# A two-layer graph kernel on one core: the front's order redrawn on all five engines

## The reference

```python
deg = max((adj != 0).sum(-1), 1)
h = relu(layernorm(x))
hs = h @ W_sa;  s_left = hs @ a_sa[0, :D];  s_right = hs @ a_sa[0, D:]
e = where(adj != 0, exp(-leaky_relu(s_left[:, None] + s_right[None, :], 0.01)), 0)
x_a = (e / (e.sum(1) + 1e-5)) @ hs
x_b = adj @ (h @ W_g) + b_g
gate_a = sigmoid(concat(adj @ h, h) @ Wa.T + ba)
gate_b = sigmoid(concat(adj @ h, h) @ Wb.T + bb)
x = x + sigmoid(gate_a * x_a + gate_b * x_b)
h = relu(layernorm(x))
dinv = rsqrt(deg)
x = x + relu((dinv * (adj + I) * dinv @ h + h) @ W1 + b1)
```

## Time and profile before

| | us |
|---|---|
| three runs | 601.46, 602.61, 606.09; median 602.61 |
| profiled execution, whole time | 602.26 |
| its span, first to last instruction | 600.5 |
| PE busy | 583.7 |
| DVE busy | 509.6 |
| ACT busy | 374.4 |
| POOL busy | 213.2 |

### The profile page before, as it was taken

How to read it: one execution, slowest core, us unless ns; L and a number is a source line. 1 busy time by engine, 2 the same in 40 slices (tenths; PEclk the granted TensorE clock), 3 DMA queues, 4 the chain that set the end, 5 groups by cost and what they waited for, 6 DMA issues and landing times.

```text
span 600.5 us, 14573 instructions
## 1 busy us (share of the span) xinstructions
PE 583.7 (97%) x5841; PEld 507.1 (84%) x5841; DVE 509.6 (85%) x965; ACT 374.4 (62%) x899; POOL 213.2 (35%) x319
## 2 busy tenths in 40 slices
PE   6889999999999999999999999999999999999996
PEld 4446778888888888888888888888888889999995
DVE  5897795999999999899989989988782999988852
ACT  3677776798979788888888879889770331000000
POOL 3655323453545444443444358223131323000001
PEclk9999999999999999999999999999999999999999
DMA  7908299776574647474756475000130266656511
GB/s 199 225 8 115 71 190 238 184 107 173 77 185 76 171 72 175 73 175 72 176 76 172 76 169 77 6 18 2 20 114 19 72 258 221 203 184 205 185 34 36
DMA packets 55807, 73.69 MB, mean 123 GB/s; under 512 B 20027, under 2 KB 47933, under 8 KB 54331
## 3 DMA queue, kind: packets, MB, share of 16 engines
q0 software_dynamic: 28544, 22.15, 26.9%
q1 hardware_dynamic: 24754, 46.42, 23.7%
q10 hardware_dynamic: 2441, 4.20, 2.5%
HBM read 69.31 MB, written 22.16 MB: 152 GB/s over the span
## 4 chain that ended last, share of the span: by engine, by line
PE 78%; DVE 6%; POOL 5%; issue 4%; DMA 4%; ACT 2%; ACTq 0%; POOLq 0%; DVEq 0%
PE accE L860 11%; PE accE L862 11%; PE accE L861 11%; PE accA L838 11%; PE accA L839 10%; PE accA L946 4%; PE accA L945 4%; DMA stage<-in_adj_dram 3%; PE accE L946 2%; PE accE L945 2%; PE accA L904 2%; PE accA L905 2%; POOL stage L420 1%; DVE bst L1052 1%; DMA late<-in_L_gnn_W_gcnb_dram 1%
## 5 line engine op out<-in xcount | busy, mean ns | idle before, releaser
L860 PE MATMUL accE<-HI,Z 128*128 128x257 f16 x676 | 184.3, 273 | 1.3 <-DVE wm L1197 0.9
L862 PE MATMUL accE<-HI,E 128*128 128x257 f16 x676 | 184.1, 272 | 0.0
L861 PE MATMUL accE<-LO,Z 128*128 128x256 f16 x676 | 183.9, 272 | 0.0
L594 ACT ACTIVATE Z<-LO,sr 128x256 f32<-128x256 f32 x338 | 151.4, 497 | 32.8 <-PE accE L862 32.8
L838 PE MATMUL accA<-HI,adjT 128*128 128x260 f16 x676 | 154.0, 273 | 0.0
L839 PE MATMUL accA<-LO,adjT 128*128 128x258 f16 x676 | 154.0, 273 | 0.0
L603 ACT ACTIVATE Z<-Z,sr 128x256 f32<-128x256 f32 x338 | 150.1, 496 | 0.2
L1153 DVE TENSOR_TENSOR Z<-adjT,Z 128x512 f32<-128x512 bf16 x169 | 126.0, 745 | 17.1 <-ACT Z L603 16.1
L1159 DVE TENSOR_TENSOR E<-Z 128x512 bf16<-128x512 f32 x169 | 128.7, 762 | 5.8
L420 POOL DMA_DIRECT2D stage<-in_adj_dram x96 | 59.3, 649 | 90.6 <-DVE adjT L1145 86.3
L860 PEld LDWEIGHTS accE<-HI,Z 128*128 128x128 bf16 x676 | 65.8, 97 | 10.5 <-issue 1.5
(11 more groups left out here) (208 smaller groups left out, 1081.7 us busy)
## 6 DMA issues: line engine op xcount, KB each, us to landing
adjT_store<-adjT SPq DMA_DIRECT2D x11, 1664.0 KB, 6.3
stage<-in_adj_dram POOLq DMA_DIRECT2D x48, 192.0 KB, 5.0
stage<-in_adj_dram POOLq DMA_DIRECT2D x36, 224.0 KB, 5.1
adjT<-adjT_store SPq DMA_DIRECT2D x7, 896.0 KB, 5.8
adjT<-adjT_store SPq DMA_DIRECT2D x7, 768.0 KB, 7.1
stage<-adjT_store SPq DMA_DIRECT2D x4, 896.0 KB, 6.2
stage<-adjT_store SPq DMA_DIRECT2D x4, 768.0 KB, 7.0
out_dram<-late ACTq DMA_DIRECT2D x11, 256.0 KB
```

The lines of the kernel that those rows point to most:

```text
L594: ins = act.activation(Z[:, n % RING, v], slw[:, m], ACT.Relu, bias=sr99[:, t:t + 1], scale=1.0 - SLOPE)
L860: pe.matmul(dst[:, 0:D + 1], zhi, HI[:, t, 0:D + 1], start=(t == 0), stop=False)
L861: pe.matmul(dst[:, 0:D], zhi, LO[:, t, 0:D], start=False, stop=False)
L862: ins = pe.matmul(dst[:, 0:D + 1], zlo, HI[:, t, 0:D + 1], start=False, stop=(t == TILES - 1))
```

## The change

It redraws the first 90 us or so, on every engine, and leaves the sums as they are.

- **Score columns.** The four DVE reductions of W_sa with a_sa are gone, and the 256 KB load that spread a_sa. PE transposes W_sa (4), ACT copies it, PE multiplies it by a_sa's four columns (4 small matmuls), DVE copies two columns. a_sa, Wa and Wb come as 12 rows, issued by POOL.
- **One statistic a step.** `BATCHES` is gone; POOL makes the power of pair s + 3 in step s, DVE `minus_mean(s + 2)`.
- **Turns between a dense product's tiles.** PE's `dense(i)` has `turn(i + 1)` between its two tiles, and ACT and DVE take the tiles' halves one by one. `project(s)` follows dense(s). The first product (`dense_first`) begins before the weights' second halves are there. Filler matmuls go from 60 to 32.
- **W1's scale later.** The scales of W_sa, W_g and the gate rows come in one go; that of W1 in steps 14 to 17, and its halves after round 0's gates. W1's load and that of the gate biases are issued after x.
- **Gate biases early.** POOL makes `nbias` in step 5 instead of behind the issues of chunk (3,0).
- **Adjacency.** Chunk (0,0) is turned in two parts in steps 5 and 7, (0,1) in step 9, (1,0) in 11, (1,1) in 13; chunks (1,0), (1,1), (2,0) are issued in POOL's steps 8, 10, 12 (before 6, 7, 11), (2,1) behind the loop. `turn_adj(2, 0)` moves behind round 0's gates and W1's halves, `turn_adj(2, 1)` from u = 4 to u = 6 of round 1.

```diff
-            for k, w in enumerate((ba, bb)):
-                sp.dma_start(bias2[:, k:k + 1], ...).then_inc(bias_in, 16)
-            sp.dma_start(w1, W1.rearrange("(h p) o -> p h o", p=P)).then_inc(w1_in, 16)
             sp.wait_ge(wsg_in, 32)
...
             sp.dma_start(b1rep[:], bass.AP(b1.tensor, 0, [[0, P], [1, D]])).then_inc(rep_in, 16)
+            for k, w in enumerate((ba, bb)):
+                sp.dma_start(bias2[:, k:k + 1], ...).then_inc(bias_in, 16)
+            sp.dma_start(w1, W1.rearrange("(h p) o -> p h o", p=P)).then_inc(w1_in, 16)
...
@@ POOL
+            for k, w in enumerate((Wa, Wb, a_sa)):
+                pool.dma_start(wrows[4 * k:4 * k + 4, :], w.rearrange("o (r p) -> (o r) p", p=P)).then_inc(wrows_in, 16)
...
-            inv_stds(2)
             score_weight_parts()
+            inv_std(2)
+            inv_std(3)
             load_adj(0, 1)
-            loads = {6: (1, 0), 7: (1, 1), 11: (2, 0), 12: (2, 1)}
+            loads = {8: (1, 0), 10: (1, 1), 12: (2, 0)}
             for s in range(PAIRS):
                 score_parts(s)
-                if s == 0:
-                    inv_stds(3)
-                if s in (0, 1, 2, 4):
-                    inv_stds({0: 4, 1: 5, 2: 6, 4: 7}[s])
                 gate_columns(s)
+                if 1 <= s and s + 3 < PAIRS:
+                    inv_std(s + 3)
+                if s == 5:
+                    pool.wait_ge(bias_in, 32)
+                    pool.tensor_scalar(nbias[:], bias2[:], -1.0, None, ALU.mult).then_inc(nbias_ok, 1)
                 if s in loads:
                     load_adj(*loads[s])
+            load_adj(2, 1)
...
@@ ACT
-                if 0 < s < PAIRS:
-                    first_halves(s)
+                if 0 <= s - 6 < PAIRS:
+                    expo(0, s - 6)
+                if s < PAIRS:
+                    first_half(s, 0)
                 if s + 1 < PAIRS:
                     turned(s + 1)
                 if s + 2 < PAIRS:
                     norm(s + 2)
+                if s < PAIRS:
+                    first_half(s, 1)
...
@@ PE
             def dense(i):
...
                     ins.then_inc(dn_ps, 1)
+                    if e == 0 and i + 1 < PAIRS:
+                        turn(i + 1)
...
+            turn_first_weights()
             turn(0)
-            keep_busy(20)
-            for s in range(PAIRS):
+            spread_weights(accE, 0, 3, 1)
+            score_columns()
+            keep_busy(8)
+            turn(1)
+            dense_first()
+            project(0)
+            for s in range(1, PAIRS):
                 dense(s)
...
+                project(s)
                 if s >= 6:
                     neighbours(0, s - 6)
                 if s >= 7:
                     unit(0, s - 7)
-                if s + 1 < PAIRS:
-                    project(s + 1)
...
@@ DVE
             for s in range(1, PAIRS + 6):
+                if s < PAIRS:
+                    second_half(s, 0)
+                if s + 2 < PAIRS:
+                    minus_mean(s + 2)
+                if s + 1 < PAIRS:
+                    turned_second(s + 1)
                 if s < PAIRS:
                     take_scores(s)
+                if s + 3 < PAIRS:
+                    row_stats(s + 3)
+                if s < PAIRS:
+                    second_half(s, 1)
...
-            turn_adj(2, 0)
             gate_args(0)
             gates(0)
+            second_weights(2)
+            turn_adj(2, 0)
```

More of the change, by code:

```diff
@@ L510, in _ @@
             load_adj(3, 0)
-            pool.wait_ge(bias_in, 32)
-            pool.tensor_scalar(nbias[:], bias2[:], -1.0, None, ALU.mult).then_inc(nbias_ok, 1)
             with_bias(0)
@@ L801, in widen_first, with dense_first @@
                           stop=True).then_inc(wide, 1)
+            def dense_first():
+                pe.wait_ge(whi_ok, 2)
+                pe.wait_ge(hTh_ok, 1)
+                for e in range(2):
+                    rows = slice(e * P, (e + 1) * P)
+                    for h in range(HALVES):
+                        pe.matmul(bank(dn, e), hTh[:, 0, h, rows], wh[:, h], start=(h == 0), stop=False)
+                    pe.wait_ge(hTl_ok, 1)
+                    for h in range(HALVES):
+                        pe.matmul(bank(dn, e), hTl[:, 0, h, rows], wh[:, h], start=False, stop=False)
+                    pe.wait_ge(wlo_ok, 2)
+                    for h in range(HALVES):
+                        ins = pe.matmul(bank(dn, e), hTh[:, 0, h, rows], wl[:, h], start=False,
+                                        stop=(h == HALVES - 1))
+                    ins.then_inc(dn_ps, 1)
             def dense(i):
-                if i == 0:
-                    pe.wait_ge(wlo_ok, 2)
                 pe.wait_ge(hTl_ok, i + 1)
                 for e in range(2):
-                    if i >= 1:
-                        pe.wait_ge(lo_ok, 2 * i - 1 + e)
+                    pe.wait_ge(lo_ok, 2 * i - 1 + e)
                     rows = slice(e * P, (e + 1) * P)
@@ L1057, in row_stats, with minus_mean @@
                 ins.then_inc(stats, 1)
-            def minus_mean(n):
-                a, b = BATCHES[n]
-                dve.wait_ge(rstd_ok, n + 1)
-                dve.scalar_tensor_tensor(out=nmr[:, a:b], in0=mv[:, a:b, :, 0], scalar=-1.0, in1=rstd[:, a:b],
+            def minus_mean(i):
+                dve.wait_ge(rstd_ok, i + 1)
+                dve.scalar_tensor_tensor(out=nmr[:, i], in0=mv[:, i, :, 0], scalar=-1.0, in1=rstd[:, i],
                                          op0=ALU.mult, op1=ALU.mult).then_inc(nmr_ok, 1)
             def score_weights():
-                dve.wait_ge(wsg_in, 32)
-                dve.wait_ge(arep_in, 16)
-                for h in range(HALVES):
-                    for k, dst in enumerate((w6[:, 3, h:h + 1], w6[:, 0, h:h + 1])):
-                        dve.tensor_tensor_reduce(out=prod[2 * h + k], in0=wsg[0][:, h, :],
-                                                 in1=arep[:, k * D:(k + 1) * D], scale=1.0, scalar=0.0, op0=ALU.mult,
-                                                 op1=ALU.add, accum_out=dst).then_inc(wprep, 1)
+                dve.wait_ge(wscore, 1)
+                columns = pw[:, 16:20].rearrange("p (h k) -> p k h", k=2)
+                dve.tensor_copy(w6[:, 3], columns[:, 0]).then_inc(wprep, 1)
+                dve.tensor_copy(w6[:, 0], columns[:, 1]).then_inc(wprep, 1)
             def largest(k0, k1):
@@ L1234, in _ @@
             row_stats(1)
+            gate_weights()
+            largest(2, 3)
+            minus_mean(0)
             dve.wait_ge(wsg_in, 32)
             largest(0, 1)
[L1237 removed]
             largest(1, 2)
[L1239 removed]
             minus_mean(1)
[L1241 to L1243 removed]
+            on_diagonal(0, 3)
+            scales(accE, 0, 3, 1)
+            score_weights()
+            turned_second(0)
             second_weights(0)
[L1245 removed]
@@ L1278, in _ @@
                 if s in turns:
                     turn_adj(*turns[s])
+                if s == 14:
+                    dve.wait_ge(w1_in, 16)
+                    largest(3, 4)
+                    on_diagonal(3, 4)
+                if s == 17:
+                    scales(pw, 3, 4, 2)
                 if 0 <= s - 6 < PAIRS:
```

197 lines of the change are left out of this document (96 added, 101 removed).

## The result

The changed kernel took 612.83 us in the median of four executions (607.06 to 612.85), the kernel before 602.32 beside it: a ratio of 1.0144, 95% interval 1.0113 to 1.0176. It is slower by more than the 1% that a measurement of this kernel tells apart, and outside the range of the forecast. A second series of five gave 606.4 (605.13 to 615.73), ratio 1.0063 (1.0041 to 1.0085). The ratio leaves out the execution of 615.73, a slow one by its distance from the fastest.

What follows compares the result with a forecast made beforehand. PE bounds the kernel, busy 583.7 of 600.5 us, so only gaps and useless work can be won. 7.8 of the front plus 1.1, less 3.0 and 4.4, gives 1.5 (1.4 by the times): 601.0 us, range 596.0 to 608.0.

Steps and rivals of the forecast that it cites:

- the front: Up to round 1's `neighbours`: 86.5 us instead of 94.25, 7.8 us won, with dense(0) at 12.4 and dense(8) at 45.0.
- the second score store: In SP's line: 10.6 us from block 0's landing at 92.2, so block 1 is stored at 114.5 and DVE waits 6.1.
- three signs of being wrong: DVE reaching the transpositions without waiting (then (A)), a score store of 15 us or more (then (B)), dense(8) after 48 (then (C)).
- The last sum: Forecast time: 600.9 us against the profiled execution, median 0.35 above the profiled one, given as 601.0.
- round 2 at 134.2: Start of round 2, before at 135.63: `unit(1,8)` at 117.7 plus 16.5 for the rest of round 1.
- the step without `rstd`: Front, dense(3) to dense(4), 18.9 to 24.4: DVE stands at `minus_mean(4)` since POOL holds `inv_std(4)` behind issues and columns.
- the quiet price: 10.6 us for a score store, instead of the crowded 18.3; the second was taken to meet only the loads of block 3.
- DVE waits 6.1: Before block 2's transposition: DVE stands ready at 86.1 and waits 6.1 us for block 0's store, landed at 92.2.
- `unit(1,0)` at 101.0: Start of round 1's units on PE: 5.8 us earlier than before, PE having stood 3.0.
- (B): Rival: score stores share the engines with adjacency loads, block 1 landing after 115.9; 611.8 us, chance 0.14.
- (C): Rival: the front wins 4 instead of 7.8 and the line of stores starts 3.8 later; 604.8 us, chance 0.13.
- (A): Rival: the stores do not bind, most of the front's gain arrives; 593.5 us, 596.5 with the first store binding; chance 0.14.

Runs made afterwards that it cites:

- experiment 3: Changed kernel, SP's wait kept, with each block's store issued ahead of the score store that stood in front of it: 604.7 us, ratio 1.0029.
- experiment 1: Changed kernel without SP's wait for chunk (1,1): 603.68 us, ratio 1.0011; its second run, the same kernel again for its profile, 603.72 us.
- experiment 9's second run: Changed kernel, with POOL issuing chunk (2,1) only when (2,0) has landed: 608.23 us, ratio 1.0116.
- experiments 1, 3 and 6: 6: changed kernel, `with_bias(0)` ahead of the issues of (3,0), (2,0) and (3,0) turned later: 606.89 us; also without SP's wait, 600.28 us.
- experiment 9's first run: Changed kernel, with SP waiting for block 0's store to have landed before it issues the second score store: 605.81 us, ratio 1.0068.
- experiment 5: Changed kernel with the adjacency load and turn tables of the kernel before; `turn_adj(2, 0)` and `turn_adj(2, 1)` keep their later places: 595.95 us, ratio 0.9893.
- experiment 4: Kernel before with the adjacency part of the change alone, plus nbias early, which it needs: 611.04 us, ratio 1.0131.

## Why the prediction was wrong, step by step

**The bound and the place were right.** Time went where the forecast said: DVE at the transpositions (2,0) and (3,0), PE ahead of `unit(1,0)` and in the middle of round 1 (128 for the forecast 113 to 118). Nothing happened in the stretch behind round 2. What failed were the sizes of the front and of the second score store, and an input of `turn_adj(2, 0)` that had no term. Two of its three signs of being wrong came up: a score store of 15 us or more (25.9) and dense(8) after 48 (48.43). (The last sum has a slip: 600.9 and 0.35 make 601.25, not 601.0.) The one number, round 2 at 134.2, came out 146.23, 12.0 later, and it adds up by the chain of its own terms:

| term | forecast | measured | later by |
|---|---|---|---|
| chunk (1,1) issued | 61.6 | 65.31 | 3.7 |
| its landing, first score store issued | + 8.1 | + 8.8 | 0.7 |
| first score store | 10.6 | 12.2 | 1.6 |
| block 0 landed, after the read's issue | 11.9 | 12.9 (to 99.3) | 1.0 |
| second score store, from block 0's landing | 10.6 | 14.1 | 3.5 |
| read and block 1's store | 11.7 | 11.6 (to 125.0) | -0.1 |
| transposition, mask, split | 3.2 | 3.2 (to 128.25) | 0 |
| rest of round 1 | 16.5 | 18.0 | 1.5 |

**The front (7.8 forecast, 3.75 measured): the step that failed first.** It failed in two of its terms. Dense(0) was taken at 12.4 and came at 14.94. In the same front it came at 12.58 in the run of experiment 3 and at 12.26 in the second run of experiment 1:

```profile
12.58 0.60 PE L834 MATMUL accA<-wh,hTx 128*128 128x512 f16 x2
```

The next pair came 0.44 us after the first here (13.02), and 0.85 after it in the changed kernel's profile (14.94 to 15.79). So PE's matmuls went at half pace up to then, and the fillers and turns ahead of them took nearly twice as long (eight fillers 1.89 us for 1.05, four turns 1.06 for 0.60 to 0.66). The clock column reads 1.00 there all the same; in the profile of experiment 9's second run, with dense(0) at 14.12 and the same long fillers, it reads 0.50 from 9 to 14 us. So this term of 2.5 us was sound by its mechanism and met an execution with a late clock; the start also varies in the old front (13.93, 13.14 and 15.15 in three profiles).

An early start did not bring the forecast front either. In three of the four profiles with dense(0) at 12.26 to 12.58 (experiments 1, 3 and 6), dense(8) still came at 47.23 to 47.58: after PE's stop of 1.9 to 2.0 us for `rstd` the clock fell inside dense(3), and the step to dense(4) took 5.36 us where it takes 3.73 at the full clock.

```profile
24.98:30.34 5.36, 5.36 (x27) 2.97 (x28) 3.48 (x11) 3.73 (x8) 1.95 (x7) 0.68 1.28 226
```

Only the fourth (experiment 9's first run) kept the clock and had dense(8) at 45.73, so 45.0 was never reached. The rest in the changed kernel's profile is small misses: dense(0) to dense(4), with the step without `rstd` in it (5.36 for the forecast 5.5), took 16.24 for 15.7; dense(4) to dense(8) 17.25 for 16.9; dense(8) to `neighbours(1,0)` 42.07 for 41.5. Together 4.0. Over all profiles, `neighbours(1,0)` began at 89.7 (mean of the ten with this front and these tables, 87.80 to 90.69) against 95.6 (three with the old): 5.9, and experiment 5 gives 6.1 us of time. I would now say 6.

**The stores.** The first score store's price was nearly right (12.2 for 10.6). "I take the quiet price ... the second meets only the loads of block 3" was wrong: it is issued 0.75 us behind block 0's store, and the loads of (2,0) and (2,1) were still on their way. It took 25.9 us, 14.1 of them behind block 0's landing, where the sum has 10.6. I counted it from that landing, as if the one began when the other ended; experiment 9 shows that they move at once, and that kept apart the second takes 11.5, near my quiet price, which it never had in the changed kernel.

**Chunk (2,0).** The forecast had no term for it. It was 24 us on its way, where chunk (1,1), with nothing beside it, took 8.8 (65.31 to 74.13). Experiment 1 shows that it alone holds DVE to 96.0. This is what the sentence "DVE waits 6.1" missed: when one of two inputs is made early, the other decides. In the changed kernel itself the two came 0.2 us apart, so the missing term cost next to nothing there; it shows as soon as the stores are early.

**`unit(1,0)` at 101.0, measured 109.47.** 7.3 us of it is the landing at 99.5 for 92.2. Most of the other 1.2 is POOL: `with_bias`, behind the four issues of (3,0), ended at 108.33 (107.07 and 1.26), while `rsg`, had it taken the 0.16 of the kernel before and not 0.91, would have let `wm` start at 107.64 but for `with_bias`. "Row sums 1.5" was read as DVE's own work.

**The clock.** No term either; 2.8 us behind the hole, hidden by the store, and 1.5 us in the rest of round 1 (granted 0.62 from 128.25 to 131 and 0.78 from there to 134, behind the second stop), where nothing hid it.

**The rivals.** (B), 611.8 by block 1 landing after 115.9, is what happened, with 125.0; its mechanism (score stores slowed by adjacency loads) is not shown: the first took 12.2 us beside eight loads, and in experiment 9 the second took 11.5 beside those of (3,0). What slowed the second goes with the block store beside it. That the time came so near (B)'s is in part luck. (C), the front giving less, came on top. The chances of 0.14 and 0.13 were too small together: they do not exclude each other, and both push the same line of stores, one late event adding to the next. (A) was wrong for this kernel. In the kernel of experiment 5 no store binds, and it takes 595.95, not (A)'s 593.5 for that case, as the front gives 6.1 and not 8.8; (A)'s other figure, 596.5, was for a first store that binds, so its nearness is luck.

**What of the change pays.** The redrawn front with nbias early, W1 later: 6.1 us, by experiment 5. The adjacency tables: 8.4 lost in the old kernel (experiment 4, with the later places of two transpositions), 10.4 in the new (experiment 5, tables alone, against the second series). What stays open is why the changed kernel's executions lie at 605 to 608 or at 613 to 616; both of its profiles are of the late kind (612.84 and 615.73). Block 1's store was the last event in both (125.05, 126.65), and in experiment 9's run with the score store alone, of 604.03, DVE turned (3,0) at 117.28. That fits, but no profile of a quick execution of the changed kernel shows it.

## What to carry to other kernels

When a front gets faster, look at what its steps trigger: a transfer whose issue is tied to a step number, and every queue behind its landing. List every input of the instruction that will wait, with when each lands, not only the one that is last in the old profile. And put what PE needs soonest (here the masks, row sums and `with_bias`) ahead of a wait on its engine: that turned 7.3 us of idle time into 1.05 with no transfer moved, though the whole gained less, since the next late chunk stopped the engine instead.

## What the runs showed of the hardware

- A store of 6 KB in 4-byte pieces took 10.2 to 12.2 us wherever no block store ran beside it, with loads of chunk (2,0) beside it or not, and 15.8 to 26.4 (27.9 in the execution of 615.73) with a block store (1664 KB) beside it or just ahead. The block store goes with the long ones; by what mechanism no run shows.
- Two stores of SP issued 0.65 us apart ended together after 19.5 us, where one after the other takes 23.1; adjacency loads ran beside them, but one chunk at a time. In the changed kernel, with two chunks beside them at once, the block store was done after 12.6 us and the score store after 26.6.
- With the same front, the first dense product began anywhere from 12.26 to 15.11 us in ten profiles, by when PE's matmuls took up the full pace.
- After the hole of 7.3 us PE ran its units at the level of 1.2 GHz for 5.8 us. In the front a stop of 1.9 to 2.0 us was followed by a fall of the clock in four profiles of ten (granted 0.68 over the next step, which took 5.35 or 5.36 us) and one of 1.7 to 2.0 by none in the six others (3.73).
- DVE's `rsg`, 0.16 us elsewhere, took 0.90 or 0.91 in each of the seven profiles where it began during POOL's sum of 1.26, and ended with it (107.44 + 0.91 = 108.35, against 107.07 + 1.26 = 108.33 in the changed kernel). A small DVE instruction can be held by a POOL one whose result it doesn't read.
